# Selective scan with a quantised feed-forward on one core: a new order of the loads in SyncE's queue, and three ScalarE copies one step later

## What is computed

```python
def step(h, inp):                       # 1024 channels, 16 states, fp32
    xt, dtt, Bt, Ct = inp
    dA = jnp.exp(dtt[:, :, None] * A[None])
    h = h * dA + (dtt * xt)[:, :, None] * Bt[:, None, :]
    y = jnp.einsum('bds,bs->bd', h, Ct)
    return (h, y)
...
xn = _layernorm(x, axis=-1)
x = x + mamba(xn, ...) + fp4_ffn(xn, ...)
```

## Time and profile before

| | |
|---|---|
| median of 3 runs | 5356.45 us (5354.84 to 5357.74) |
| the profiled execution's own time | 5352.76 us |
| its span, first to last instruction | 5351.0 us |
| phase_b in it | from about 1776 to 5351 us |
| chunks in the steady part | one in about 220 us |
| granted TensorE clock, mean | 0.976 of full speed |

### The profile page before, as it was taken

The page is one execution under the profiler, slowest core; times in us unless marked ns, Lnnn a source line. Parts: engine busy times, 40 slices in busy tenths (PEclk is TensorE's granted clock), DMA queues, the critical chain, the costliest instruction groups (busy, mean ns, idle before and its releaser), DMA issues.

```text
span 5351.0 us, 80535 instructions
## 1 busy us (share of the span) xinstructions
PE 4918.7 (92%) x22532; PEld 3287.7 (61%) x22532; DVE 4686.7 (88%) x5835; ACT 2777.2 (52%) x4594; POOL 3950.9 (74%) x2047
## 2 busy tenths in 40 slices
PE   5899999999999799899999999989999999999967
PEld 2688888888888455555555555555555555555544
DVE  9676766767676699999999999999999999999997
ACT  3111111111111576777677677777667776767754
POOL 5233333333332599999999999999999999999996
PEclk9999999999999899999999999999999999999979
DMA  4111111111110423323233333333333333323222
GB/s 117 48 44 41 45 39 45 41 43 43 39 47 32 128 88 111 102 92 108 87 122 101 91 104 110 98 102 94 115 95 99 107 92 111 110 81 114 80 91 66
DMA packets 286369, 444.72 MB, mean 83 GB/s; under 512 B 39521, under 2 KB 100961, under 8 KB 281746
## 3 DMA queue, kind: packets, MB, share of 16 engines
q1 hardware_dynamic: 285970, 440.23, 26.2%
HBM read 350.94 MB, written 89.17 MB: 82 GB/s over the span
## 4 chain that ended last, share of the span: by engine, by line
DVE 18%; PE 17%; issue 14%; ACT 8%; POOL 7%; DVEq 1%; DMA 1%; SPq 0%; POOLq 0%; ACTq 0%
DVE hs L1434 11%; DVE acc L1448 6%; POOL v L1193 5%; PE mm L1567 4%; PE ht L1579 4%; ACT decay L1392 3%; PE mm L1508 3%; PE mm L1499 3%; PE mm L1516 2%; POOL hw L1203 1%; PE yw L1589 1%; PE mm L1551 1%; DVEq L1019 1%; DMA b_rep<-ssm_d 1%; ACT L1279 1%
## 5 line engine op out<-in xcount | busy, mean ns | idle before, releaser
L1193 POOL TENSOR_TENSOR v<-u,b_rep 128x1024 f32<-128x1024 f32 x1024 | 2401.2, 2365 | 150.2 <-DVE hs L1434 68.1
L1392 ACT ACTIVATE decay<-dt,a_neg 128x512 f32<-128x512 f32 x2048 | 1389.7, 688 | 657.0 <-DVE hs L1434 644.7
L1579 PEld LDWEIGHTS ht<-ident,hs 128*128 128x128 f32 x6400 | 784.8, 144 | 1013.9 <-issue 662.6
L1434 DVE TENSOR_TENSOR_SCAN hs<-decay,carry,v 128x512 f32<-128x512 f32 x1024 | 1285.2, 1273 | 34.9 <-POOL hw L1203 19.5
L1434 DVE TENSOR_TENSOR_SCAN hs<-decay,v 128x512 f32<-128x512 f32 x1024 | 1230.6, 1221 | 49.2 <-ACT decay L1392 38.3
L1448 DVE SCALAR_TENSOR_TENSOR acc<-ht,c_now,acc 128x512 f32<-128x512 f32 x1600 | 1173.3, 733 | 17.4 <-PE ht L1579 16.5
L1579 PE MATMUL ht<-ident,hs 128*128 128x128 f32 x6400 | 1005.0, 281 | 179.3 <-DVE hs L1434 83.6
L683 ACT ACTIVATE sg<-gate 128x512 f32<-128x512 f32 (+1 forms) x192 | 108.1, 563 | 1339.9 <-PE up L723 1339.9
L1203 POOL TENSOR_TENSOR hw<-hs,c_rep 128x512 f32<-128x512 f32 x448 | 572.1, 1277 | 10.4 <-DVE hs L1434 10.4
L1567 PE MATMUL mm<-w_out,yt 128*128 128x512 f32 x1024 | 513.0, 605 | 8.7 <-ACT xb L1264 5.2
L1516 PE MATMUL mm<-w_in,x_z 128*128 128x512 f32 x1024 | 508.6, 601 | 6.7 <-ACT acc L1318 6.7
(11 more groups left out here) (157 smaller groups left out, 7971.0 us busy)
## 6 DMA issues: line engine op xcount, KB each, us to landing
b_rep<-ssm_d SPq DMA_DIRECT2D x512, 256.0 KB, 3.5
w_out<-in_L_attn_W_out SPq DMA_DIRECT2D x32, 1024.0 KB, 7.8
rtb<-res_d SPq DMA_DIRECT2D x128, 256.0 KB, 4.1
tap_diag<-tap_d SPq DMA_DIRECT2D x120, 256.0 KB, 3.5
c_rep<-ssm_d SPq DMA_DIRECT2D x448, 64.0 KB, 3.4
xt<-in_L_attn_x SPq DMA_DIRECT2D x64, 256.0 KB, 2.7
xn_d<-xn SPq DMA_DIRECT2D x64, 256.0 KB, 2.0
rt<-in_L_attn_x SPq DMA_DIRECT2D x64, 256.0 KB, 2.6
```

Source lines behind the costliest of these rows:

```text
L1193: nc.gpsimd.tensor_tensor(v[k % 2][:, j:j + 2, :], u[g][:, j:j + 2, :], b_rep[k % 3][:, :].unsqueeze(1).broadcast_to([P, 2, CL]), ALU.mult ...
L1392: nc.scalar.activation(decay[n % 3][:, :], dt[g][:, j, :], ACT.Exp, scale=a_neg[:, GD * g + j, s:s + 1]).then_inc(decay_ready, 1)
L1434: nc.vector.tensor_tensor_scan(h[k % 3][:, j, :], decay[n % 3][:, :], v[k % 2][:, j, :], carry[:, s, GD * g + j:GD * g + j + 1] if c.secon ...
L1579: last = nc.tensor.transpose(ht[add_no[k, t] % 2][:, j, :], h[k % 3][:, j, t * P:(t + 1) * P], ident[:, :])
```

## The change

In every slot `part` now takes two kinds of entries out of their place, `row` (the load of a block of x into `x_row`) and `x_store`, and issues them last in the slot, behind the loads of C and of B. `x_store` moves from slot 1 to slot 3. In slot 27 the load of the residual stands ahead of the row. In ACT_AT the copies of `ip` 6, `z` (0, 2) and `z` (1, 0) each come one step (n) later. Nothing is added or removed.

```diff
-              54: [("xd", 1, 3)], 57: [("cv", 4)], 60: [("ip", 6)], 63: [("cv", 5)], 66: [("ip", 7)],
+              54: [("xd", 1, 3)], 57: [("cv", 4)], 61: [("ip", 6)], 63: [("cv", 5)], 66: [("ip", 7)],
...
-    SP_AT = {1: [("x_store",)], 2: [("w_out", 1), ("load", 1, 0), ("load", 1, 1)], 5: [("tap", 2)], 7: [("tap", 3)], 8: [("store", 1, 0)],
+    SP_AT = {2: [("w_out", 1), ("load", 1, 0), ("load", 1, 1)], 3: [("x_store",)], 5: [("tap", 2)], 7: [("tap", 3)], 8: [("store", 1, 0)],
...
         def part(c):
             for k in range(SLOTS):
+                turns = [what for what in SP_AT.get(k, ()) if what[0] in ("row", "x_store")]
                 for what in SP_AT.get(k, ()):
-                    move(c, *what)
+                    if what not in turns:
+                        move(c, *what)
                 if c.exists(NC) and k in weigh_no:
                     load_c(c, k)
...
                 elif c.plus(1).exists(NC):
                     load_b(c.plus(1), k + 2 - SLOTS)
+                for what in turns:
+                    move(c, *what)
```

More of the change, by code:

```diff
@@ L965, in phase_b @@
              20: [("load", 0, 0), ("load", 0, 1)], 21: [("tap", 1)], 23: [("ssm",)], 25: [("row", 0), ("store", 0, 0)],
-             26: [("store", 0, 1), ("load", 0, 2)], 27: [("row", 1), ("load", 0, 3)], 28: [("store", 0, 2)], 29: [("row", 2), ("store", 0, 3)],
+             26: [("store", 0, 1), ("load", 0, 2)], 27: [("load", 0, 3), ("row", 1)], 28: [("store", 0, 2)], 29: [("row", 2), ("store", 0, 3)],
              31: [("row", 3), ("x_z",)]}
```

## The result

The changed kernel takes 5408.1 us (median of 5 runs, 5406.37 to 5411.19); the kernel before, timed beside it, 5354.84 us (5 runs, 5354.04 to 5357.74). That is 53.3 us more, a ratio of 1.0098 with a 95% interval of 1.0087 to 1.0109. The prediction was 5430 us, +75.7 us, range 5395 to 5455: the sign, the place and the range held, the size was over by about 22 us. The profiled execution took 5411.19 us, 58.4 us over the one of before; its span is 5409.4 us.

The account below looks back on a forecast made before the run. DVE, busy 215.2 of 220 us a chunk, bounds the kernel, so stalls reaching it lengthen it. Late block 3 adds 38.7 us at nine chunk ends and 37 at five loop turns: +75.7 us, 5430 us, range 5395 to 5455.

Parts of the forecast that it names:

- Part 1: Rows of blocks 0 to 2 behind B's loads: POOL's wait in slot 29 goes, worth 0 us; bounds -16 and 0.
- Part 2: Block 3 of x, in slot 31 behind `x_z`: late for PE and DVE at 14 chunk ends, 38.7 + 37 us.
- The landing: Block 3 lands 8.3 us after `x_z` is issued, queued behind its 1 MB and `b_rep`; lower end 4.6 us.
- `tr` 3 and `ht` at half clock with the signal: After block 3 lands, PE's transposes and last `ht` take 1.1 us each, plus 0.1 us for the signal.
- The second wait of DVE in the new chunk: DVE's 0.60 us wait for `hw` early in the next chunk goes, leaving net +4.3 us at 9 chunk ends.
- The five turns of the loop: Chunk ends where the loop turns back: +7.4 us each, 5 times, 37 us; 6.3 us each if the pause shrinks.
- Part 3: `x_store` from slot 1 to slot 3: nobody waits for the `b_rep` it stood ahead of, 0 us.
- Part 4: Three ACT copies a step later: DVE has no wait there, 0 us; bounds -0.2 and +0.2 us a chunk.
- Rival A: Block 3's row does not queue behind `x_z`, landing 4.6 us after it; 14 us in all, 5370 us; chance 0.06.
- Rival B: Faster: POOL's waits for B set DVE's pace, chunk-end pauses cover late block 3; 5335 us; chance 0.04.
- Rival C: PE stays at half clock after idling, DVE waits 2 us more at each of 14 ends; 5460 us; chance 0.08.
- The pause at the loop's turn: At loop turns DVE pauses 3.14 us and PE 6.20 us without work they wait for; these pauses move whole.

## Why the prediction was right, and where its sizes were off

**What bounds the kernel.** Right. DVE is the full engine, and its own waits set the time: with PE's wait for block 3 shortened by two different means, the time fell by about as much.

**Part 1, blocks 0 to 2: 0 us.** Right, in value and in reason: the wait moved from slot 29 to slot 1.

**Part 2, block 3.** The mechanism held at each step; its two terms were too large.
- The landing: 8.3 us after `x_z` was predicted, 7.4 us is what PE shows (2468.95 against 2461.52) and 7.3 at the loop's turn. Two things are in it: POOL could start on `b_rep` 6.9 us after `x_z` (2468.39), where it had been 7.6 before, and block 3 was there 0.56 us behind it, where I had allowed 0.9. In all 0.9 us at 14 ends, 12 us of the error. The landings that the term was built on (6.3 and 6.0 us) were measured with `x_store`'s megabyte issued right behind them; the change takes it away, and with `x_store` alone moved the same load takes 5.2 us. At the loop's turns this does not explain it: there `x_store` came later before as well, and why the loads landed sooner than 8.3 us is open. The Trainium skill's fit for another issuing path ("DMA: Bandwidth & Descriptors", section "Anatomy of one DMA") gave an estimate of 5.8 us for the full `x_z` ahead; the measured 7.4 us decides.
- `tr` 3 and `ht` at half clock with the signal: 2.3 us predicted, 2.0 measured (2468.95 to 2470.95). The 1.12 us for four transposes are as predicted. 4 us in all.
- The second wait of DVE in the new chunk: I said that the 0.60 us for `hw` go. They do, but 0.65 us for `decay` stand there in their place, behind ACT's silu. The net at this end is +3.7 us and not +4.3. Over the nine ends of this kind, from one `x_z` to the next, it is +2.1 to +5.0 us, 3.4 on average.
- The five turns of the loop: +5.2 us at the first (222.45 us from `x_z` to `x_z` against 217.21), +5.0 to +5.8 at the five, 5.5 on average, where 7.4 was predicted. DVE's pause moves nearly as a whole, as assumed, but is 2.90 us and not 3.14; the landing and `tr` 3 with `ht` take off another 1.3 us, so the first scan comes 5.9 us later (12.9 against 7.0), and 0.6 us of that are made up within the chunk.

Nine times 3.4 and five times 5.5 make 58 us, the difference of the two profiled executions; the medians of the runs differ by 53.3. So 17 of the 22 us are the terms above, and the other 5 are that the profiled execution of before was below its median and that of the changed kernel the slowest of its five.

**Part 3, x_store: 0 us.** Wrong by a small term. The step that failed is that a transfer costs only those who wait for what stands behind it in the queue. In its old place it slowed the two loads of B issued just ahead of it: 6.3 us to land for the first, 5.2 without it. Moved alone it is worth 6.8 us (2.7 to 12). In the changed kernel this gain does not come on top: with all moves +53.3 us, with block 3 alone +55.8. There the late `tr` 3 holds `x_store` back to 9.1 us behind `x_z` even in slot 1, and the load of B ahead of it lands in 5.4 us, so the late block 3 does by itself what the move to slot 3 does.

**Part 4, the copies: 0 us.** Right.

**Rival A** (the row meets no queue) fell: PE had the row 7.4 us after `x_z`'s issue, and even with only a quarter of `x_z` ahead PE still waited 5.6 us for it, where 4.6 us from `x_z`'s issue to the landing had been the rival's figure. **Rival B** fell for this change. A gain of its size was there to be had: with `x_z` behind the loads of B the kernel takes 5333.5 us, where B said 5335. That the figures meet is luck, for 12.8 of the 22.5 us come from that order, and DVE's waits for `hw`, from which B took its 22.7 us, fell only to 12.5. The change moved the rows of x behind B and left the one entry that holds B, `x_z`, in front. **Rival C** (PE stays behind) is not seen. The granted clock after the wait at the end of chunk 2 is in the column before the last two:

```profile
2471.00:2473.00 2.00, 2.00 (x10) 1.61 (x9) 2.00 (x3) 0.96 (x3) 2.00 (x1) 0.50 1.05 403
...
2475.00:2477.00 2.00, 2.00 (x9) 1.04 (x8) 2.00 (x3) 1.99 (x2) 1.60 (x1) 1.00 0.37 108
```

It is the lower of the clock's two levels until 2473 and the full one from 2475, 6 us after `tr` 3 began; at the loop's first turn it is full from 2706, some 10 us after. No further wait for `ht` of that size follows.

**The pause at the loop's turn.** The prediction said that the profile shows no work that DVE and PE waited for there; for PE that is what the row says. DVE's row names `decay`; but the new chunk's first `decay` was done at 2680.94, 1.8 us before DVE started, so the reading holds in substance.

## What to carry to other kernels

In a queue that works in order, ask of each entry first what its wait is for, and only then how long its transfer takes. An entry that waits for a product of the current stage makes everything behind it late; a load whose consumer stands directly behind that product must be ahead of it. Put the waiting, far-ahead transfer (here `x_z`, read 67 steps later) where its condition has long been met. A large transfer can also slow the loads issued just ahead of it, as `x_store` did. And when POOL's waits for a buffer vanish in one place, look whether they come back in the next before counting them as won.

## What the runs showed of the hardware

Where the loop turns, PE and ACT pause with nothing that they wait for in the profile ("issue"): PE 6.20 us, ACT 3.85 us before the new chunk's first `decay` at the first turn of the kernel before:

```profile
2680.25 0.69 ACT L1392 ACTIVATE decay<-dt,a_neg 128x512 f32<-128x512 f32 x1 [3.85 <-issue]
```

The place of `x_z` matters for it. ACT's pauses of this kind in phase_b, first with `x_z` issued at the chunk end (behind the loads of B and block 3), then with `x_z` alone moved to slot 4:

```profile
ACT decay L1396 <- issue: 19.0, 5, 3.9
```

```profile
ACT decay L1392 <- issue: 11.8, 5, 2.5
```

PE's pause at the first turn is 6.14 us in the one and 3.75 us in the other, where the profile names DVE's last addition. Whether it is the megabyte on the move is not settled. In the changed kernel PE gets to its last instruction only after that megabyte has landed, and its pause is 2.36 us, but DVE still paused 2.90 us; and with a quarter of `x_z` ACT's pause at the first turn was still 3.36 us. The page lists transfers of kind "instruction" among the DMA queues (q8, 150 packets, 2.46 MB), so instructions that have to share the DMA engines would explain it; no run here shows it directly.
